# Expert stage: 39 slots with one expert each against 36 slots, four of them shared by two experts

## The reference, cut to what matters

```python
xn = rms_norm(x, norm_scale)
scores = einsum('bsd,ed->bse', xn, w_router)          # 8 experts
_, ids = top_k(scores, 2); probs = softmax(scores)
val, gate = split(einsum('bsd,ehd->bseh', xn, w_up), 2)   # H = 704
y = einsum('bseh,edh->bsed', val * silu(gate), w_down)
out = x + sum over the token's two experts of probs * y
```

## Time and profile before

| | before |
|---|---|
| median of three runs | 421.85 us |
| the profiled execution's own time | 421.26 us |
| its span, first to last instruction | 419.4 us |
| PE busy | 375.3 us, 89% |
| DVE, ACT, POOL busy | 265.6, 242.4, 180.3 us |
| stages A and B (until the first routing operation) | 0 to 138.9 us |
| routing until the first expert matmul | 138.9 to 161.1 us |
| expert stage to the last scatter's start | 161.1 to 411.1 us |
| from there to the end of the span | 8.3 us |

### The profile page before, as it was taken

The page is one execution under the profiler, slowest core; times in us unless marked ns, Lnnn a source line. Parts: engine busy times, 40 slices in busy tenths (PEclk is TensorE's granted clock), DMA queues, the critical chain, the costliest instruction groups (busy, mean ns, idle before and its releaser), DMA issues.

```text
span 419.4 us, 9669 instructions
## 1 busy us (share of the span) xinstructions
PE 375.3 (89%) x2491; PEld 268.6 (64%) x2492; DVE 265.6 (63%) x672; ACT 242.4 (58%) x451; POOL 180.3 (43%) x184
## 2 busy tenths in 40 slices
PE   5699999999998066999899999999999999999981
PEld 5578888888886042566466666666666666666650
DVE  2799678898886986877766664454445445445440
ACT  3499965877765386778556544545444444454440
POOL 2545545765556002346345444334434434433321
PEclk9899999999999659999999999999999999999998
DMA  7999873452225602143243343334334343333411
GB/s 226 404 423 409 317 242 113 135 167 76 76 83 195 193 1 64 28 65 63 53 76 57 57 77 58 68 65 68 58 63 71 55 74 65 55 72 63 63 16 24
DMA packets 45302, 47.57 MB, mean 113 GB/s; under 512 B 25696, under 2 KB 41056, under 8 KB 44128
## 3 DMA queue, kind: packets, MB, share of 16 engines
q1 hardware_dynamic: 37200, 36.28, 26.8%
q0 software_dynamic: 7536, 10.52, 15.9%
q10 hardware_dynamic: 544, 0.52, 0.4%
HBM read 32.83 MB, written 9.50 MB: 101 GB/s over the span
## 4 chain that ended last, share of the span: by engine, by line
PE 71%; ACT 8%; DVE 8%; issue 5%; DMA 4%; POOL 1%; POOLq 0%; SPq 0%; DVEq 0%; ACTq 0%
PE bank L1339 32%; PE bank L1366 5%; PE bank L1390 5%; PE bank L1391 5%; PE bank L1392 5%; ACT arena L464 3%; PE bank L1200 3%; PE bank L1254 3%; PE bank L1263 2%; ACT arena L479 2%; DMA arena<-in_w 2%; PE bank L1142 1%; PE bank L1151 1%; PE bank L1160 1%; PE bank L1158 1%
## 5 line engine op out<-in xcount | busy, mean ns | idle before, releaser
L1339 PE MATMUL bank<-expert_w,arena 128*128 x702 | 152.0, 362 | 3.9 <-issue 1.1
L772 POOL DMA_INDIRECT out<-arena,add_idx x39 | 67.5, 1732 | 128.1 <-ACT arena L646 128.1
L1339 PEld LDWEIGHTS bank<-expert_w,arena 128*128 128x128 f16 x702 | 66.9, 98 | 65.1 <-issue 12.1
L761 POOL DMA_INDIRECT arena<-xrow_hbm,take_idx x39 | 40.0, 1026 | 42.8 <-DVE add_idx L1055 22.6
L1116 DVE SCALAR_TENSOR_TENSOR arena<-bank,dn_small,arena 128x512 f32<-128x512 f32 x78 | 45.3, 580 | 18.5 <-PE bank L1339 15.9
L1103 DVE COPY arena<-bank 128x1024 f16<-128x1024 f16 x39 | 26.9, 690 | 44.0 <-PE bank L1366 44.0
L668 ACT ACTIVATE arena<-arena 128x512 f16<-128x512 f32 x39 | 24.5, 629 | 51.7 <-DVE arena L1116 51.7
L1390 PE MATMUL bank<-expert_w,arena 128*128 x195 | 53.2, 273 | 1.0 <-DVE arena L1103 0.9
L1391 PE MATMUL bank<-expert_w,arena 128*128 x195 | 53.2, 273 | 0.0
L1392 PE MATMUL bank<-expert_w,arena 128*128 x195 | 53.2, 273 | 0.0
L1122 DVE TENSOR_TENSOR arena<-arena 128x512 f16<-128x512 f32 x39 | 27.0, 693 | 28.4 <-ACT arena L668 28.4
(11 more groups left out here) (191 smaller groups left out, 679.4 us busy)
## 6 DMA issues: line engine op xcount, KB each, us to landing
expert_w<-in_wup SPq DMA_DIRECT2D x8, 1408.0 KB, 18.0
expert_w<-in_wdn SPq DMA_DIRECT2D x8, 640.0 KB, 4.7
rows<-in_x SPq DMA_DIRECT2D x8, 256.0 KB, 7.5
arena<-in_ctxT SPq DMA_DIRECT2D x8, 256.0 KB, 3.2
xrow_hbm<-front SPq DMA_DIRECT2D x8, 256.0 KB, 2.3
out<-rows SPq DMA_DIRECT2D x8, 256.0 KB, 2.7
rows<-in_wup SPq DMA_DIRECT2D x1, 1408.0 KB, 6.0
expert_w<-in_wdn SPq DMA_DIRECT2D x16, 64.0 KB, 4.5
```

What stands on the lines that cost most here:

```text
L761: pool.indirect_dma_start(out=xs_row[:, i % 2], out_offset=None, in_=xrow_hbm, in_offset=bass.IndirectOffsetOnAxis(ap=take_idx[:, i:i + 1] ...
L772: pool.indirect_dma_start(out=out, in_=yt[:, i % 2], in_offset=None, out_offset=bass.IndirectOffsetOnAxis(ap=add_idx[:, i:i + 1], axis=0), ...
L1339: last = T.matmul(bank[q][:, 0:n], xsT[:, slot, 2 * a + c], up_w[:, ds(w0 + c * UPC + w * 2 * H + lo, n)], start=m == 0, stop=m == len(pro ...
```

## The change

The slots become 36: 32 uniform ones of 128 pairs of one expert, and 4 mixed ones in which partitions 0 to 63 belong to one expert and 64 to 127 to another. An expert with a remainder of up to 64 pairs beyond its full tiles uses a half slot. Experts are ordered by their number of full tiles, the largest first.

- Because the order is known only after routing, nothing is split in stage B. The largest expert is split after the counts, from where it was loaded. The seven others are fetched again from HBM by DMAs that ACT issues inside the expert stage, and split there (`FETCH_UP`, `FETCH_DN`, `UP_STEP`, `DN_STEP`).
- All down weights are loaded once by SP right behind the up weights. The 16 up squares stay in stage A, two in a step, the 8 down squares are in stage B, one in a step. One matmul sums both, and one POOL operation takes 16 inverse roots instead of two with 8.
- `xrow` has two buffers. The softmax's reciprocal and product move from DVE to POOL.
- The routing chain has 24 operations instead of 10 between the counts and `in_tile`, and 11 after `add_idx` for the tables of slots and homes. DVE makes 25 of the 32 `in_col`, ACT 7 (24 and 8 before).
- A mixed slot's two halves use two sets of weights: each matmul becomes two with 64 stationary columns. The second half's split weights are copied inside SBUF by DMAs of ACT (2 for up, 1 for down per slot), and each mixed slot is scattered by two indirect DMAs, one after the other.
- All loops over expert steps are written out; there is no hardware loop in that stage.

```diff
-NSLOT = 2 * NT + NE - 1
+UNIFORM, MIXED = 2 * NT, NE // 2
+NSLOT = UNIFORM + MIXED
...
-        FRONT = 4
-        UP_SLOT = {1: 8, 2: 9, 3: 10, 4: 11, 5: 12, 6: 13, 9: 14, 11: 15}
-        DN_SLOT = {1: [6], 2: [7], 3: [8], 4: [9], 5: [10], 6: [11, 12], 7: [13], 10: [14], 12: [15]}
+        FIRST_SLOT = [0, 4, 7, 11, 14, 18, 21, 25]
+        UP_STEP = {2: (1, 0), 3: (1, 1), 5: (2, 0), 6: (2, 1), 8: (3, 0), 9: (3, 1), 11: (4, 0), 12: (4, 1),
+                   14: (5, 0), 15: (5, 1), 17: (6, 0), 18: (6, 1), 20: (7, 0), 21: (7, 1)}
+        DN_STEP = {3: (1, 0), 4: (1, 1), 6: (2, 0), 7: (2, 1), 9: (3, 0), 10: (3, 1), 12: (4, 0), 13: (4, 1),
+                   15: (5, 0), 16: (5, 1), 18: (6, 0), 19: (6, 1), 21: (7, 0), 22: (7, 1)}
+        FETCH_UP = {1: 1, 2: 2, 5: 3, 8: 4, 11: 5, 14: 6, 17: 7}
+        FETCH_DN = {2: 1, 3: 2, 6: 3, 9: 4, 12: 5, 15: 6, 18: 7}
+        HALF_STEP, MIX_STEP = 24, 27
...
+            def up_high(k, c, e):
+                if k:
+                    act.wait_ge(s_lo, 2 * k + 2)
+                    act.wait_ge(s_fup[k], 16)
...
+            def fetch_up(k, e):
+                act.wait_ge(s_lo, 4)
+                act.dma_start(expert_w[:, (k + 1) * EXP:(k + 1) * EXP + UPC], wup[ds(e, 1)].squeeze(0)).then_inc(s_fup[k], 16)
+            def fetch_down(k, e):
+                act.wait_ge(s_dlo, 2)
+                dst, src, tail = raw_dn(k + 1), wdn[ds(e, 1)].squeeze(0), (NH - 1) * D
+                act.dma_start(dst[:, 0:tail], src[:, 0:tail]).then_inc(s_fdn[k], 16)
+                for lo in (0, HLAST):
+                    act.dma_start(dst[lo:lo + HLAST, tail:DNC], src[0:HLAST, tail:DNC]).then_inc(s_fdn[k], 16)
...
+                if r == HALF_STEP:
+                    act.wait_ge(s_lo, 2 * NE + 2)
+                    act.wait_ge(s_dlo, 2 * NE)
+                    for q in range(2):
+                        copy_half_up(q)
+                        copy_half_down(q)
...
-                pool.indirect_dma_start(out=out, in_=yt[:, i % 2], in_offset=None,
+                for m in range(1 if i < UNIFORM else 2):
+                    if i == UNIFORM and not m:
+                        pool.wait_ge(s_half, 3)
+                    if i or m:
+                        pool.wait_ge(s_add, added(i) + 16 * m)
...
-            steps(pe, step_e, *E_STEPS)
+            steps(pe, step_e, NSLOT + 3, NSLOT + 3, NSLOT + 3)
```

More of the change, by code:

```diff
@@ L618, in _ @@
             act.wait_ge(s_rtr, NBATCH)
+            for slot in range(2):
+                act.wait_ge(s_row[slot], 16 * NBATCH // 2)
             for n in range(DVE_COLS, 2 * NT):
@@ L1087, in _ @@
[L1087 to L1097 removed]
+            link(V.tensor_reduce(rank, ahead[:, 0], AX.X, ALU.add))
@@ L1126, in step_e @@
                     if r == 1:
-                        load_expert("pair", 1)
-                        scale_pairs(it, k)
-                    if r in UP_SLOT:
-                        low_parts([UP_SLOT[r]])
-            steps(dve, step_e, *SPLIT_E_STEPS)
+                        expert[1] = scale_pairs(1)
+                        for h in range(2):
+                            down_low(0, h, first)
+                    if r in UP_STEP:
+                        n, c = UP_STEP[r]
+                        up_low(n, c, load_expert(slot_expert, UNIFORM + 2 * MIXED + n))
+            steps(dve, step_e, NSLOT + 3, NSLOT + 3, NSLOT + 3)
         @block.tensor
@@ L1376, in step_e @@
+                if r == 1:
+                    load_next_home(1)
                 if live(r, 2, NSLOT):
[L1377 to L1385 removed]
```

746 lines of the change are left out of this document (398 added, 348 removed).

## The result

The changed kernel takes **467.04 us** (median of 4 runs, 464.09 to 467.83), the kernel before beside it 421.22 (4 runs, 420.56 to 421.88): ratio **1.1075**, interval 1.102 to 1.113. The prediction was 427.5 with a range of 411 to 440: slower was right, the size was not. The profiled execution took 467.83 with a span of 465.9, so 46.5 more than before in the span where the forecast had 6.1. The rest of this document looks for the other 40.4 us.

A forecast was written before the change was run, and what follows sets the result against it. PE was taken as the bound, busy 375.3 of 419.4 us. First transposes 169.3 + 193.3 for 32 steps + 8.4 + 7.8 + 2.0 + 1.0 + 0.8 = 382.6, plus 42.9 of scatters: span 425.5, time 427.5 us, range 411 to 440.

The forecast's parts named there:

- Stages A and B: Before routing: waits and splits taken out against POOL's inverse root and DVE's constants put in; -1.0 us, bounds -4 to +2.
- Routing: From the counts to the first expert matmul: 24 short DVE operations instead of 10 make that matmul 2.8 us later.
- First fetch: Expert steps 1 to 3: ACT waits for expert 1's weights and issues DMAs; 8.4 us, bounds 3 to 12.
- The other splits: Steps splitting experts 2 to 7: DVE's late product 4.8, ACT's issues 3.0; sum 7.8 us, bounds 3 to 14.
- Half copies: Step 24: ACT issues six DMAs and four register loads, some 4.5 us, half of it hidden; costs 2.0 us.
- the hole and the slack: In a step: ACT idle 1.6 us, and about 0.35 us slack from DVE's product to the next transposes.
- Tables: Four expert steps with six small DVE copies each; costs 1.0 us.
- Mixed slots on PE: Mixed slots' matmuls: a pair of 64-column matmuls takes the time of one; 0.8 us for a slot.
- the rival of serial halves: Mixed slots: the halves run one after the other, 11.4 us a slot instead of 6.8; 441 us, chance 0.14.
- The last scatters: From the first mixed transposes to the end: POOL's scatters, 4.0 us each, set the end; 42.9 us.
- the contention rival: Expert stage and end: fetches and copies share DMA engines with gathers and scatters, slowing them; 438 us, chance 0.13.
- the hidden stalls: ACT in steps 1 to 24: fetches, splits, copies and tables cost 7 instead of 19.2; 415 us, chance 0.28.

The follow-up runs named there:

- kernel 17: Changed kernel with four buffers for gathered rows and the gather issued six slots ahead instead of four: 467.5 us, ratio 1.1067.
- experiment 2: Changed kernel with expert numbers written in the program instead of ACT's and DVE's register loads (other weights, another output): 442.5 us.
- 6: Changed kernel with one register load per expert on ACT and DVE, down split and mixed scales behind the products: 451.87 us, ratio 1.0746.
- experiment 4: Changed kernel with no fetches, no half copies and no waits for them, register loads kept (another output): 436.55 us, ratio 1.035.
- experiment 8: Changed kernel with one scatter for each mixed slot instead of two (some rows can be added wrongly): 453.23 us, ratio 1.0755.
- kernel 13: Kernel 10 with four buffers for the transposed rows too, and half copies issued later: 429.33 us, ratio 1.0159.
- kernel 16: Kernel 13 with the gather issued six slots ahead instead of four and the later mixed slots at 31 and 33: 407.28 us, ratio 0.9677.
- experiment 5: Changed kernel with fetches, half copies and their register loads in SP's list instead of ACT's: 463.79 us, ratio 1.1017.
- 12: Kernel 10 with ACT instead of SP issuing fetches and half copies: 434.71 us, ratio 1.0313.
- 10: Changed kernel with stage B reordered, SP issuing fetches and copies, few register loads, mixed slots early, four gathered-row buffers: 428.24 us, ratio 1.0154.
- experiment 1: Changed kernel with stage B reordered: scores before squares, five down loads behind context loads, constants after the last xn: 464.8 us, ratio 1.1023.

## Why the prediction was wrong, by its own steps

- **Stages A and B, -1.0 (bounds -4 to +2):** +3.8, outside. "In the middle of the stage PE's own work fills the steps" failed: the order in ACT's and SP's lists was costed at nothing. The constants were seen (2.5, measured 3.0), the scores behind the squares and the context behind the down loads were not.
- **Routing, +2.8 at the first expert matmul:** 3.8 (168.66 less 161.13, less the 3.8 above). The 24 operations took 6.3 as forecast (147.94 to 154.25). The forecast's 0.7 back in the first step did not come (168.66 to 175.94 is 7.28, before 7.06). Mechanism right, size 1.9 off.
- **First fetch, 8.4 (3 to 12):** 10.6, inside, but by parts 5.3, 2.8 and 2.4 against 3.7, 2.2 and 2.5, and only the first came in the way that was forecast: ACT waited 5.40 for the DMA, PE 4.04 for ACT. The 2.8 was the clock of 0.50 behind that wait, which had no term; ACT's late start lay under it (in kernel 17, at a clock of 1.00, PE waits 1.89 for ACT there). The 2.4 was three issues and a load in ACT's list, for which PE waited 1.76 (L670); the down weights' landing, which the forecast had there, held nothing, since L584 stood 0.34 at issue and for no DMA. That the last two sizes agree is luck.
- **The other splits, 7.8 (3 to 14):** 20.8. This is the largest miss, and the step that failed is the pricing of register loads: one was counted at 0.47 from ACT's copy L646, and none on DVE. The trace has 0.63 in the mean ahead of each down split on the chain, which by the forecast's own reckoning had 0.35 of slack; experiments 2 and 6 take 10 us out of this stretch, experiment 4 the 8.8 of the issues. The issues were on the list (3.0), at a third of their cost. The two prices are not a sum that must add up to 20.8, since late rows lie beside both; kernel 17, without late rows, loses as much here (some 1.7 of it is a clock of 0.50 for 3.4 us), so the lists alone account for nearly all of it.
- **Half copies, 2.0:** 9.6. "Half of it in the hole and the slack" was wrong, since six DMAs in a row fit no hole, and the loads between them took 1.3 each beside the copies; 4.5 us of list was 9.4 from the first issue to ACT's next copy (346.00 to 355.41).
- **Tables, 1.0:** 5.7, of which 5.5 were the eight loads (experiment 2).
- **Mixed slots on PE, 0.8:** 0.7 to the first mixed transposes. Right; the rival of serial halves is excluded by the rows. The Trainium skill, "TensorEngine Tiling (Array Packing)", Key Properties, has tiles independent, and the pairs agree. Its Restrictions take the fast weight load from column tiling; the trace has 0.11 us for a load of 64 columns and 0.10 for one of 128, so half the columns take no less time, which agrees with a slower load. It cost nothing to be seen: a pair followed the pair before it after 0.21, and the slots' intervals were 6.25 and 6.26.
- **The last scatters, 42.9:** 49.3, and 43.9 without half copies (experiment 4). The 4.0 apart was right where nothing ran beside them (436.75 to 440.76); the term that was missing is the copies beside the scatters, 5.4, and the contention rival was right for the first two. PE's path was 4 too long: it had 17.6 behind the last transposes, and experiment 8 measured 12.5.
- **Rivals:** the hidden stalls (faster) were wrong for the reason that was written against them. Contention (438) had the right places, the scatters and the steps with fetches; but in the changed kernel the bytes cost only the first fetch, a part of the copies and the end, and in the steps with fetches they began to cost once the lists were short (13.7 us between kernels 13 and 16). None of the four cases reached 467, since all priced ACT's and DVE's lists from the same too small rows.

What stays open: how much of each stall is the lower clock behind it, since no run holds the clock up by itself; how loads, issues and the down split's place divide the 20.8, since each experiment takes out one in the presence of the others; and how the 8.6 us of kernel 16 outside intervals 4 to 22 divide between the lead and the positions.

## What to carry to other kernels

Before moving work onto the fly, write down each engine's list for one step with everything in it: register loads and DMA issues stand in the same order as the computing, and a chain with a third of a microsecond of slack pays most of each. Load a number once, where the engine has work to cover it, and give transfers to a queue whose engine does not compute, if what already stands in that queue has lead enough (it gave 3 us in experiment 5, 6.5 between 12 and 10). When a step has late input, look for the instruction that waits first and at the list that issues its DMA; buffers alone give no lead if the issue stands behind something else. Repairs can hide each other: the gather's lead bought nothing in the changed kernel and some 14 us once the lists were short.

## What the runs showed of the hardware

- A register load from SBUF on ACT, with the register operations behind it, made a gap of 0.65 us between two DMA issues, and of 1.3 while copies of 704 KB inside SBUF ran.
- Two 64-column matmuls on disjoint halves of the array started within 0.01 us of each other, and the next pair 0.21 later; a slot made of such pairs took 6.26, one of single matmuls 6.04.
- In kernel 13 four gathers issued beside a fetch of 1408 KB landed after 6.7 to 7.0 us; the median of all 36 is 3.5.
- After PE had stood still for 2.33 us (experiment 1) the granted clock was 0.50, the lower of its two levels, for some 3 us, and the interval was 3.3 longer than in the changed kernel, the wait included. After 4.04 us of standing still (the changed kernel) it was 0.50 for 6.8 us, and PE did 12 matmuls in 4.68 us instead of 2.43.
